# Three of four half tiles transposed by VectorE and put in place by SBUF transfers; two late features looked up on TensorE

## The reference

```python
e = jnp.stack([tbl_0[ids[:, 0]], ..., tbl_26[ids[:, 26]]], axis=1)        # (2048, 27, 128)
interactions = jnp.einsum('bnd,bmd->bnm', e, e)
z = interactions[:, i, j]                                                 # i, j = triu_indices(27, k=1)
h = jnp.concatenate([z.reshape(2048, -1), dense_ctx], axis=1)             # (2048, 367)
h = jnp.maximum(h @ W_top1 + b_top1, 0.0)                                 # 512 wide
h = jnp.maximum(h @ W_top2 + b_top2, 0.0)                                 # 256 wide
y = h @ W_top3
```

## Time and profile before

| | |
|---|---|
| median of 3 runs (lowest, highest) | 347.62 us (347.22, 347.96) |
| span of the profiled execution | 346.3 us |
| TensorE clock granted | 1.0 in all slices |
| busy: PE, PEld, DVE | 331.1, 282.8, 219.4 us |
| busy: ACT, POOL | 184.7, 242.9 us |
| DMA packets, bytes | 53981, 44.06 MB |

### The profile page before, as it was taken

One profiled execution on the slowest core, in us unless ns is written; L12 is line 12 of the kernel. 1 busy time (PEld: TensorE's weight loads), 2 busy tenths in 40 slices (PEclk: granted clock), 3 DMA queues, 4 the chain that ended last, 5 costly groups with the idle time before them and its releaser, 6 DMA issues.

```text
span 346.3 us, 8212 instructions
## 1 busy us (share of the span) xinstructions
PE 331.1 (96%) x3478; PEld 282.8 (82%) x3478; DVE 219.4 (63%) x160; ACT 184.7 (53%) x315; POOL 242.9 (70%) x263
## 2 busy tenths in 40 slices
PE   2899999999999999999999999999999999998995
PEld 1667878887898888887898889887888889997894
DVE  5899997599427971499626991399724990360021
ACT  4898975533646354633646355633447346554521
POOL 6777777777777777777777777777777777777200
PEclk9999999999999999999999999999999999999999
DMA  6975795655237772768229772677327552572440
GB/s 169 222 178 168 225 252 142 156 157 135 67 55 157 146 158 55 107 173 178 83 55 157 146 160 55 89 197 177 83 57 134 131 112 57 85 168 72 85 81 8
DMA packets 53981, 44.06 MB, mean 127 GB/s; under 512 B 39810, under 2 KB 43983, under 8 KB 53945
## 3 DMA queue, kind: packets, MB, share of 16 engines
q1 hardware_dynamic: 43993, 26.52, 35.1%
q0 software_dynamic: 8192, 16.79, 21.3%
q10 hardware_dynamic: 1760, 0.22, 0.4%
HBM read 36.43 MB, written 7.09 MB: 126 GB/s over the span
## 4 chain that ended last, share of the span: by engine, by line
PE 86%; DMA 6%; SPq 3%; ACT 2%; issue 1%; DVE 1%; DVEq 0%
PE emb_ps L572 21%; PE emb_ps L574 20%; PE gram_ps L600 16%; PE mlp_ps L617 11%; PE mlp_ps L626 7%; PE emb_ps L583 7%; DMA h<-tbl_rows 3%; DMA products<-gram 1%; DMA gram<-tbl_rows 1%; PE emb_ps L644 1%; SPq L376 1%; DMA z<-products 1%; SPq L369 1%; PE mlp_ps L671 1%; PE mlp_ps L655 1%
## 5 line engine op out<-in xcount | busy, mean ns | idle before, releaser
L543 POOL DMA_INDIRECT rows<-tbl_rows,idx x256 | 242.0, 945 | 78.9 <-issue 74.4
L747 DVE TENSOR_TENSOR onehot<-ids_b,row_id 125x2048 fp32r<-125x2048 int32 x72 | 158.9, 2279 | 33.3 <-PE emb_ps L574 33.3
L572 PE MATMUL emb_ps<-onehot,table_hi 125*128 125x512 f32 (+1 forms) x400 | 147.6, 378 | 5.6 <-DVE table_lo L768 4.0
L574 PE MATMUL emb_ps<-onehot,table_lo 125*128 125x512 f32 (+1 forms) x400 | 143.0, 367 | 0.0
L572 PEld LDWEIGHTS emb_ps<-onehot,table_hi 125*128 125x128 f32 x400 | 76.0, 190 | 21.5 <-DVE table_lo L768 4.8
L574 PEld LDWEIGHTS emb_ps<-onehot,table_lo 125*128 125x128 f32 x400 | 76.1, 190 | 10.7
L600 PEld LDWEIGHTS gram_ps<-emb 128*54 128x54 f32 x2048 | 53.6, 130 | 5.6 <-issue 3.5
L600 PE MATMUL gram_ps<-emb 128*54 128x54 f32 x2048 | 55.8, 214 | 1.7 <-ACT emb L852 0.8
L851 ACT COPY held<-emb_ps 128x256 f32<-128x256 f32 x38 | 14.1, 371 | 75.9 <-PE emb_ps L574 75.8
L784 DVE TENSOR_TENSOR mlp_ps<-mlp_ps,rows 128x256 f32<-128x256 f32 x14 | 6.1, 433 | 76.5 <-PE mlp_ps L626 76.5
L882 ACT COPY gram<-gram_ps 118x432 f32<-118x432 f32 x64 | 33.2, 519 | 39.5 <-PE gram_ps L600 39.2
(11 more groups left out here) (49 smaller groups left out, 102.6 us busy)
## 6 DMA issues: line engine op xcount, KB each, us to landing
ids_b<-ids_onehot SPq DMA_DIRECT2D x33, 256.0 KB, 5.5
products<-gram SPq DMA_DIRECT2D x28, 216.0 KB
gram<-tbl_rows SPq DMA_DIRECT2D x9, 480.0 KB
rows<-tbl_rows,idx POOLq DMA_INDIRECT x256, 2.9
z<-products SPq DMA_DIRECT2D x14, 126.0 KB
h<-tbl_rows SPq DMA_DIRECT2D x2, 480.0 KB
z<-products SPq DMA_DIRECT2D x7, 112.0 KB
w_sb<-w SPq DMA_DIRECT2D x1, 768.0 KB, 5.8
```

What stands on the lines that cost most here:

```text
L543: pool.indirect_dma_start(out=rows[:, t, f, :], out_offset=None, in_=gathered_tables[f], in_offset=bass.IndirectOffsetOnAxis(ap=idx[:, p, ...
L572: nc.tensor.matmul(ps[:, 0:width], table_hi[0:ROWS, k, j, :], columns[:, c, :], start=j == 0, stop=False)
L574: last = nc.tensor.matmul(ps[:, 0:width], table_lo[0:ROWS, k, j, :], columns[:, c, :], start=False, stop=j == ROWS_PER - 1)
L747: nc.vector.tensor_tensor(onehot[0:ROWS, seq % ONEHOT_RING, 0:own * width].rearrange("p (j b) -> p j b", b=width), *operands, ALU.is_equal ...
```

## The change

- For pairs 1 to 7 three of four half tiles (two banks of `turn` each) are turned in another way: both halves of tile 0 and the first of tile 1 (`is_flipped`). VectorE transposes their 32 x 32 blocks (`flip_half`, two instructions of up to 128 x 512 into `flips`), SP moves the blocks between partitions by 16 transfers of 32 x 1 KB (`move_half`, from `flips` to `moved`), and ScalarE copies `moved` to `emb` (`take_half`, one instruction of 128 x 1024). `flips` and `moved` have one buffer each. The second half of tile 1, and all of pair 0, stay on TensorE.
- `rows` becomes a ring of 5 banks of four features, where it had 8; a gather waits for the bank five before it, and the `keep_back` waits of pairs 2 to 7 go.
- TensorE's order after the lookups becomes: layer 1, products of tile 0, the two `turn`, layer 2, products of tile 1, in cycle 7 too.
- SP's order in a cycle changes, see below; the id slots become four, `dense` one.
- For pairs 6 and 7 the features 24 and 25 are no longer gathered. Their tables are loaded in cycle 6 into `h1` and split into the table memory of two features that are no longer needed (`round_late`, `split_late`); two more lookups of two pieces each are made in cycle 6. Their ids are laid out in DRAM at the start (`store_late_ids`).

```diff
+LATE_FEATURES = [24, 25]
+LATE_PAIR = PAIRS - 2
 LOOKUPS = [(0, 0, 2), (1, 0, 1), (1, 1, 2), (0, 2, 2), (1, 3, 2), (0, 4, 2), (1, 5, 2), (0, 6, 2),
+           (2, LATE_PAIR, 2), (1, 7, 1)]
-IDS_SLOTS = 5
+IDS_SLOTS = 4
+ROW_BANKS = 5
+HALF_BANKS = 2
+def is_flipped(p, t, n):
+    return p > 0 and (t == 0 or n < HALF_BANKS)
+PIECES_BEFORE_FLIP = [0] + [8] * (PAIRS - 2) + [6]
+LATE_SPLITS = [6, 9]
+HALF_AFTER = 4
+LATE_ROUNDS = [2, 4]
...
-        rows = sb("rows", [P, TILES, NG, DIM])
+        rows = sb("rows", [P, ROW_BANKS, TURNS_A_BANK, DIM])
+        flips = sb("flips", [P, BLOCKS, HALF_BANKS, TURNS_A_BANK, BLOCK])
+        moved = sb("moved", [P, BLOCKS, HALF_BANKS * TURNS_A_BANK, BLOCK])
...
+            def move_half(p, t, h):
+                number = HALF_NUMBER[(p, t, h)]
+                sp.wait_ge(flipped, FLIPPED_BY[(p, t, (h + 1) * HALF_BANKS - 1)])
+                if number > 0:
+                    sp.wait_ge(half_placed, number)
+                for q in range(BLOCKS):
+                    for b in range(BLOCKS):
+                        sp.dma_start(
+                            moved[b * BLOCK:(b + 1) * BLOCK, q, :, :].rearrange("p f j -> p (f j)"),
+                            flips[q * BLOCK:(q + 1) * BLOCK, b, :, :, :].rearrange("p g f j -> p (g f j)")
+                        ).then_inc(half_moved, 16)
+            def load_late_table(n):
+                if n == 0:
+                    sp.wait_ge(mlp_full, (LATE_PAIR - 1) * MLP_CHUNKS)
+                else:
+                    sp.wait_ge(late_split, n)
...
+            for p in range(1, PAIRS):
+                ids, ahead = lookups_of(p)[IDS_SLOTS:], lookups_of(p + 1)[:IDS_SLOTS] if p < LAST else []
+                if p == LATE_PAIR:
+                    load_late_table(0)
+                for i in ids[0:2]:
+                    load_ids(i)
+                store_products(p - 1)
+                move_half(p, 0, 1)
+                if p == LATE_PAIR:
+                    load_late_table(1)
+                load_z(p - 1)
+                load_dense(p)
+                for i in ids[2:]:
+                    load_ids(i)
+                for i in ahead[0:2]:
+                    load_ids(i)
+                move_half(p, 1, 0)
+                for i in ahead[2:]:
+                    load_ids(i)
+                if p < LAST:
+                    move_half(p + 1, 0, 0)
                     store_y(p - 1)
...
@@ TensorE
-                    for m in range(M1):
-                        layer1(p - 1, m)
-                        turn(p, 1, m)
...
+                gram_products(p, 0)
+                if p > 0:
+                    for n in range(HALF_BANKS, TURN_BANKS):
+                        turn(p, 1, n)
                     layer2(p - 1)
                 gram_products(p, 1)
...
@@ VectorE
+            def flip_half(p, t, h):
+                number = HALF_NUMBER[(p, t, h)]
+                if number > 0:
+                    dve.wait_ge(half_moved, number * HALF_MOVED)
...
+                for g in range(HALF_BANKS):
+                    n = h * HALF_BANKS + g
+                    dve.wait_ge(gathered[t][n], rows_gathered(p, n))
+                    nc.vector.transpose(flips[:, :, g, 0:size, :].rearrange("p b f j -> p f b j"),
+                                        row_bank(p, t, n).rearrange("p f (b i) -> p f b i", b=BLOCKS)
+                                        ).then_inc(flipped, 1)
...
                 for i, part in pieces[:ONEHOT_RING]:
                     make_onehot(i, part)
+                flip_half(p, 0, 0)
...
-                for i, part in pieces[ONEHOT_RING:]:
+                for at, (i, part) in enumerate(pieces[ONEHOT_RING:], ONEHOT_RING):
+                    if at == ONEHOT_RING + 1:
+                        flip_half(p, 0, 1)
+                    elif at == PIECES_BEFORE_FLIP[p]:
+                        flip_half(p, 1, 0)
+                    if p == LATE_PAIR and at in LATE_SPLITS:
+                        split_late(LATE_SPLITS.index(at))
                     make_onehot(i, part)
+                if PIECES_BEFORE_FLIP[p] >= len(pieces):
+                    flip_half(p, 1, 0)
...
@@ ScalarE
+            def take_half(p, t, h):
...
+                act.wait_ge(half_moved, (number + 1) * HALF_MOVED)
...
+                nc.scalar.copy(emb[:, t, :, first:first + size].rearrange("d (q j) f -> d q j f", j=BLOCK),
+                               moved[:, :, 0:size, :].rearrange("d q f j -> d q j f")).then_inc(half_placed, 1)
...
                 place_held(p)
+                if p > 0:
+                    take_half(p, 0, 0)
                 for at, i in enumerate(cycle_lookups(p)):
+                    if p > 0 and at == HALF_AFTER:
+                        take_half(p, 0, 1)
+                    if p == LATE_PAIR and at in LATE_ROUNDS:
+                        round_late(LATE_ROUNDS.index(at))
...
                     for m in range(M1):
                         take_layer1(chunk, m)
-                        take_turned(p, 1, m)
+                    take_half(p, 1, 0)
...
+                take_gram(p, 0)
...
+                    for n in range(HALF_BANKS, TURN_BANKS):
+                        take_turned(p, 1, n)
                 take_gram(p, 1)
```

More of the change, by code:

```diff
@@ L58, with emb_slot, held_place @@
 ONEHOT_RING = 3
[L62 to L65 removed]
+LATE_FEATURES = [24, 25]
+LATE_SLOT = GATHERED.index(LATE_FEATURES[0])
+LATE_PAIR = PAIRS - 2
+LATE = [NO + n for n in range(len(LATE_FEATURES))]
+SETS = [list(range(NO // 2)), list(range(NO // 2, NO)), LATE]
+LOOKUPS = [(0, 0, 2), (1, 0, 1), (1, 1, 2), (0, 2, 2), (1, 3, 2), (0, 4, 2), (1, 5, 2), (0, 6, 2),
+           (2, LATE_PAIR, 2), (1, 7, 1)]
+HELD = len(LATE) + len(SETS[0])
+IDS_SLOTS = 4
+def emb_slot(k):
+    return NG + k if k < NO else LATE_SLOT + k - NO
+def held_place(k):
+    first = SETS[1][0] if k in SETS[1] else LATE_SLOT - NG
+    return (k if k < NO else emb_slot(k) - NG) - first
 EMB_BANKS = 3
@@ L71, with bank_features, bank_number @@
 TURN_BANKS = -(-NG // TURNS_A_BANK)
+ROW_BANKS = 5
+HALF_BANKS = 2
+BLOCK = 32
+BLOCKS = P // BLOCK
+def bank_features(p, n):
+    end = min((n + 1) * TURNS_A_BANK, LATE_SLOT if p >= LATE_PAIR else NG)
+    return n * TURNS_A_BANK, end - n * TURNS_A_BANK
+def is_flipped(p, t, n):
+    return p > 0 and (t == 0 or n < HALF_BANKS)
+def bank_number(p, t, n):
+    return (p * TILES + t) * TURN_BANKS + n
+ALL_BANKS = [(p, t, n) for p in range(PAIRS) for t in range(TILES) for n in range(TURN_BANKS)]
+TURNED = [bank for bank in ALL_BANKS if not is_flipped(*bank)]
+FLIPPED = [bank for bank in ALL_BANKS if is_flipped(*bank)]
+FLIPPED_HALVES = [(p, t, n // HALF_BANKS) for p, t, n in FLIPPED if n % HALF_BANKS == 0]
+TURNED_BY = {bank: n + 1 for n, bank in enumerate(TURNED)}
+FLIPPED_BY = {bank: n + 1 for n, bank in enumerate(FLIPPED)}
+PIECES_BEFORE_FLIP = [0] + [8] * (PAIRS - 2) + [6]
+LATE_SPLITS = [6, 9]
+HALF_AFTER = 4
+LATE_ROUNDS = [2, 4]
+HALF_NUMBER = {half: n for n, half in enumerate(FLIPPED_HALVES)}
 def list_lookups():
@@ L102, in turns_ahead @@
 def turns_ahead(p, at):
-    banks = [(t, n) for t in range(TILES if p == 0 else 1) for n in range(TURN_BANKS)]
+    banks = [(t, n) for t in range(TILES if p == 0 else 0) for n in range(TURN_BANKS)]
     n = at - (len(cycle_lookups(p)) - len(banks))
@@ L117, in list_banks @@
         if p > 0:
-            out += [("turn", p * TILES + 1, n) for n in range(TURN_BANKS)]
+            out += [("turn", p * TILES + 1, n) for n in range(HALF_BANKS, TURN_BANKS)]
     return out
@@ L313, in stored_rows, with rows_gathered, row_bank @@
             return row - pad, row - pad + STORE_ROWS, PAD - pad
[L315 to L320, removed]
+        def rows_gathered(p, n):
+            return 16 * sum(bank_features(earlier, n)[1] for earlier in range(p + 1))
+        def row_bank(p, t, n):
+            return rows[:, bank_number(p, t, n) % ROW_BANKS, 0:bank_features(p, n)[1], :]
+        HALF_MOVED = BLOCKS * BLOCKS * 16
         def pieces_by(i):
@@ L446, in _ @@
             load_dense(0)
-            load_dense(1)
+            store_late_ids()
             for i in lookups_of(1)[:IDS_SLOTS]:
                 load_ids(i)
[L451 to L462, removed]
+            move_half(1, 0, 0)
+            for p in range(1, PAIRS):
[19 more added lines that the diff above has]
+                    move_half(p + 1, 0, 0)
                     store_y(p - 1)
@@ L507, in keep_back, with free_row_bank @@
                         pool.wait_ge(gram_full, TILE_GRAMS)
[L508 to L531, removed]
+            def free_row_bank(p, t, n):
+                number = bank_number(p, t, n) - ROW_BANKS
+                if number >= 0:
+                    earlier = ALL_BANKS[number]
+                    if is_flipped(*earlier):
+                        pool.wait_ge(flipped, FLIPPED_BY[earlier])
+                    else:
+                        pool.wait_ge(turned, TURNED_BY[earlier])
             for p in range(PAIRS):
@@ L543, in _ @@
```

(10 more changed lines are left out.)

123 lines of the change are left out of this document (82 added, 41 removed).

## The result

| | before | after |
|---|---|---|
| median (lowest to highest), us | 347.51 (347.22 to 347.96) | 483.24 (481.52 to 484.94) |
| span of the profiled run, us | 346.3 | 481.4 |
| TensorE clock granted, mean | 1.0 | 0.876 |

The ratio is 1.390 (95%: 1.386 to 1.394): 39% slower. The forecast was 396, range 372 to 420. Its direction was right; it saw 48.8 of 135.7 us.

A forecast was written before the change was run, and what follows sets the result against it. TensorE held 86% of the chain, VectorE and POOL right behind. VectorE's flips, SP's moves and ScalarE's copies add 4.7 + 20.4 + 16.3 + 7.4 = 48.8 us to the 346.3 span: 395.1, median 396, range 372 to 420.

The forecast's parts named there:

- I take 0.37 (ends 0.3 and 0.55): SP's queue: each move's issue takes 0.37 us, so a half's 16 take 5.9 us.
- SP is the bound: Rival, chance 0.10: at 0.53 us an issue each half lands 2.6 us later, 20 us more in all, 417.
- So taking the turned banks out of the lookups gives nothing: Lookups: VectorE's four transposes add 2.4 us, so ten pieces end at T + 22.0 (T: cycle start), before T + 20.2.
- `take_half` 2.05 us: ScalarE's strided copy of `moved` to `emb`: 1.98 ns an element, 2.05 us for 1024, low end 1.1.
- TensorE waits 1.4 us a cycle for ScalarE's take of the products: After layer 1, ScalarE's third copy precedes its first take of the products; TensorE waits 1.4 us a cycle.
- Cycle 6, "11.1 even if nothing else is late": Cycle 6's lookups end 15.9 us later, of which four pieces and two splits are 11.1.
- The second waits, with four slots, for the piece with index 3: Cycles 1, 3, 5, 6: SP's second id load waits until T + 4.4, delaying moves; VectorE's flip waits 4.1 us.
- POOL "is not in it": POOL adds nothing to the sum: its 32 gathers of 1.25 us fit cycles of 40 us and more.
- the sum: Cycles 2 and 4 4.7, cycles 1, 3, 5 20.4, cycle 6 16.3, cycle 7 7.4: 48.8 on the 346.3 span, 395.1.
- landing after the last issue: SP's moves: a half lands 2.5 us after the last issue, nearest rows 1.8 and 3.0 us.

The follow-up runs named there:

- experiment 1: The changed kernel with the late ids given as an input of their own, without the four DRAM transfers of 4-byte elements: 451.3 us, ratio 1.300.
- experiment 3: Against experiment 1, each half moved by 9 transfers instead of 16, same bytes, exchange of blocks between partitions left out: 400.3 us, ratio 1.155.
- experiment 2: Against experiment 1, each half moved by 4 transfers of 128 x 1 KB instead of 16, exchange between partitions left out: 381.1 us, ratio 1.092.
- experiment 7: Against experiment 2, without the late features: 24 and 25 gathered in all pairs, no late tables or late lookups: 370.1 us, ratio 1.063.
- experiment 10: Against experiment 2, SP stores the products and moves half (p, 0, 1) before loading second ids in cycles 1, 3, 5, 6, 7: 385.6 us.
- experiment 9: Against experiment 2, ScalarE's copy put behind tile 0's products, no late features, and one feature of four transposed: 357.1 us, ratio 1.022.

## Why the prediction was wrong

Its steps, with what measured them:

- *"I take 0.37 (ends 0.3 and 0.55)"* for the issue of a move: failed. It measured 0.591, outside my high end. I had taken the rows of table parts, which come from DRAM. The nearest figure was the one that my rival used, a dense load's 0.53 (72.35 in the trace of before; the earlier trace rows shows only the first two, 0.72 each). The rule of the Trainium skill that I set beside it (DMA: Bandwidth & Descriptors, "Why a DMA increments its semaphore by 16 and not by 1"), an estimated 0.43 us, was closer, and still too low: the trace decides. Experiments 1, 3 and 2 show that the count of issues makes the time: 16, 9 and 4 a half give 451.3, 400.3 and 381.1. This one term is 51 us, with what the clock loses by it.
- *No term for `store_late_ids`*: failed. The four transfers stood in the change and I gave them nothing. They hold SP for 22 us, fill the DMA engines, and delay whatever comes behind: 31.9 us here, 27 alone in the kernel before, 13 even in a pause. None of my rows had a transfer of 4-byte elements, and what they don't show has to be bounded from both sides; here there was no bound, and the range had no room for it. The two terms together, 51.0 + 31.9, are 82.9 of the 86.8 us between forecast and result.
- *The rival "SP is the bound"*, 0.53 us an issue, 417: the right mechanism. Without the small transfers it would have had to give 451. It added 2.4 to 2.6 us once a cycle, and 5.2 in cycle 7. In fact both halves of a cycle come onto the path, and the queue runs over into the next: in cycle 2 (T = 149.0) the moves of (2, 0, 0) end at 150.95, the stores leave at 152.10, and the flip of (2, 1, 0) comes at T + 19.7 instead of T + 14.2.
- *"So taking the turned banks out of the lookups gives nothing"*: right, T + 22.0 in experiment 2. Two flips keep VectorE 1.22 us from the next piece (111.19 to 112.41), 0.61 each against 0.6.
- *`take_half` 2.05 us*: right, 2.03 us. The line's group in the kernel after, with VectorE's flips (busy us, mean ns, idle before):

```profile
L1014 ACT COPY emb<-moved 128x1024 f32<-128x1024 f32 x19 | 38.5, 2027 | 46.8 <-DMA moved<-flips 46.6
L903 DVE STREAM_TRANSPOSE flips<-rows 128x512 f32<-128x512 f32 x40 | 26.1, 689 | 64.6 <-DMA moved<-flips 64.6
```

  The rule of ScalarE: Activation LUTs, "What ACT_TABLE_LOAD costs" in the Trainium skill, which had this at an estimated 1.05 us, doesn't hold for such a copy; the row of `held` did.
- *TensorE waits 1.4 us a cycle for ScalarE's take of the products*: right in kind. The wait is 1.12 us; moving the copy away gave 9.8 us, 1.4 in each of seven cycles.
- *Cycle 6, "11.1 even if nothing else is late"*: right, 11.0 (experiment 7).
- *"The second waits, with four slots, for the piece with index 3"*: right; without that wait cycles 1, 3 and 5 gain 4.9 us (experiment 10).
- *POOL "is not in it"*: right for this kernel, whose gathers wait for other engines; not once the rest is short, since experiment 9's flips wait 16.1 us for gathers.

Why then does experiment 3 meet the sum, 395.1 against 395.1? Because the schedule was right. Its trace against the sum, cycle by cycle:

| cycle | 0 | 1 | 2 | 3 | 4 | 5 | 6 | 7 to the end |
|---|---|---|---|---|---|---|---|---|
| worked out, us | 62.2 | 48.4 | 39.9 | 48.4 | 39.9 | 48.4 | 53.9 | 54.1 |
| experiment 3, us | 62.7 | 48.5 | 40.3 | 47.6 | 40.5 | 48.6 | 53.9 | 52.9 |

Meeting it to the tenth is luck: that run is the fastest of four, the median is 400.3, and terms that miss offset one another (landing after the last issue taken as 2.5 us where the two waits above give 1.3 and 1.9; some halves at 6 to 7.4 us; a mean clock of 0.969, which the sum has nowhere). The range failed because I kept it to ends of terms that I knew of, and for the move's issue to an end (0.55) under what it measured.

## What to carry to other kernels

A queue that only issues can be the bound: price each new transfer by the count of its issues, with a row of the same kind (SBUF to SBUF, DRAM to SBUF), and when there is none, let the range hold twice the nearest one (here 0.35 us, measured 0.59). Transfers of single elements are not free because they are few or early: ask what is queued behind them. Work taken from the engine that holds the chain pays only as far as the next engine's cover reaches (here 0.2 to 0.6 us a cycle), and that is read from when buffers are ready, not from busy shares.

## What the runs showed of the hardware

- A transfer from SBUF to SBUF takes 0.6 us of SP's queue whether it has 32 or 128 rows of 1 KB (591 and 602 ns in the median); table parts from DRAM take 0.35.
- Four transfers of 256 elements of 4 bytes each, DRAM to DRAM, hold SP for 22 to 25 us. In the kernel after the first ids behind them landed 18.5 us after their issue, where the median of all such loads is 4.7.
- TensorE's clock falls when it is held up. From 61 to 90 us, in which it waited 11.26 us for the first piece, 0.59 of the clock was granted; the two levels are 1.2 and 2.4 GHz. The matmuls behind the wait take 0.63 us each, and 0.40 from 89.29 on. After, TensorE in order of time, then two windows (busy of the five engines, clock, DMA share, GB/s):

```profile
83.78 0.77 PE L675 MATMUL emb_ps<-onehot,table_hi 125*128 125x512 f32 x1 [11.26 <-DVE onehot L848]
...
88.19 0.63 PE L675 MATMUL emb_ps<-onehot,table_hi 125*128 125x512 f32 x1
...
89.52 0.40 PE L675 MATMUL emb_ps<-onehot,table_hi 125*128 125x512 f32 x1
```

```profile
61.00:90.00 29.00, 13.32 (x130) 10.79 (x130) 8.65 (x6) 5.51 (x7) 5.94 (x7) 0.59 0.56 59
90.00:148.00 58.00, 39.29 (x351) 32.29 (x351) 31.31 (x24) 17.82 (x28) 26.42 (x28) 0.79 0.44 115
```

  TensorE was busy for 359.0 us, 27.9 more than before, although by the prediction's count the change takes 11.6 us of work from it. The same 3338 instructions kept it busy for 350.9 us in experiment 1, 339.4 in 3 and 337.1 in 2; how much of that lies on the path isn't settled. The mean clock comes back as the waits go: 0.876, 0.905 (experiment 1), 0.969 (3), 0.978 (2).
